# A fifth group of tiles in the first edges' matrix of a graph layer, and two buffers for its turned blocks

## The reference

```python
xn = _layernorm(x, axis=-1)
gathered = edge_vals[:, None] * x[cols]                              # x is xn, cols is dst
new_x = jax.ops.segment_sum(gathered, rows, num_segments=N_NODES)    # rows is src
out1 = new_x @ hamilton1        # batch norm, tanh, then @ hamilton2
```

## Time and profile before

| | us |
|---|---|
| runs, median of 3 | 2246.98 (2240.45 to 2256.11) |
| the profiled execution | 2244.61 |
| its span | 2243.2 |
| busy: PE, DVE, POOL, ACT | 1845.0, 1600.0, 1270.8, 1122.8 |
| scatters, all 566 | first issued at 95.7, last at 1265.1 |
| stage over the nodes, then experts | from 1269 to 1537, then to the end |

### The profile page before, as it was taken

The page is one execution under the profiler, slowest core; times in us unless marked ns, Lnnn a source line. Parts: engine busy times, 40 slices in busy tenths (PEclk is TensorE's granted clock), DMA queues, the critical chain, the costliest instruction groups (busy, mean ns, idle before and its releaser), DMA issues. The chain is left out here.

```text
span 2243.2 us, 36774 instructions
## 1 busy us (share of the span) xinstructions
PE 1845.0 (82%) x10829; PEld 1543.1 (69%) x10829; DVE 1600.0 (71%) x5189; ACT 1122.8 (50%) x2255; POOL 1270.8 (57%) x811
## 2 busy tenths in 40 slices
PE   3689996778788888878886287757999999999994
PEld 1366675566566666657775146635999999999994
DVE  4666667887877877853332196777888888888883
ACT  2544453222232333332222025348888988988983
POOL 1467787788877877877777400002544544554551
PEclk7599998888888989988998598857999999999997
DMA  9978877687788888889997771343888888888885
GB/s 316 353 132 170 157 118 125 111 127 127 125 166 148 143 175 147 154 171 189 178 181 120 144 252 60 122 142 85 240 228 240 227 231 241 226 233 236 232 234 159
DMA packets 326116, 401.84 MB, mean 179 GB/s; under 512 B 34999, under 2 KB 267468, under 8 KB 325778
## 3 DMA queue, kind: packets, MB, share of 16 engines
q1 hardware_dynamic: 194048, 257.05, 36.9%
q0 software_dynamic: 103008, 103.83, 34.6%
q10 hardware_dynamic: 28850, 38.50, 5.3%
HBM read 251.13 MB, written 154.55 MB: 181 GB/s over the span
## 5 line engine op out<-in xcount | busy, mean ns | idle before, releaser
L1143 POOL DMA_INDIRECT acc_dram<-third x566 | 905.3, 1599 | 275.3 <-issue 143.4
L2077 POOL DMA_INDIRECT sum_dram<-node,small x112 | 195.9, 1749 | 314.2 <-DVE node L2006 297.2
L563 PE MATMUL bank<-work,third 128*128 128x256 f32 x1132 | 308.3, 417 | 45.2 <-ACT third L1097 41.6
L1947 PE MATMUL bank<-down_parts 128*128 128x256 f32 x2688 | 335.4, 284 | 0.0
L1934 PE MATMUL bank<-up_parts 128*128 128x256 f32 x2688 | 333.1, 284 | 2.3 <-DVE up_parts L1964 2.3
L1934 PEld LDWEIGHTS bank<-up_parts 128*128 128x128 f32 x2688 | 327.9, 193 | 2.7 <-DVE up_parts L1964 2.7
L1947 PEld LDWEIGHTS bank<-down_parts 128*128 128x128 f32 x2688 | 325.3, 191 | 0.0
L1097 ACT ACTIVATE third<-bank 128x512 f32<-128x512 f32 x283 | 168.3, 597 | 287.0 <-DMA acc_dram<-third 219.9
L563 PEld LDWEIGHTS bank<-work,third 128*128 128x128 f32 x1132 | 228.2, 214 | 84.2 <-ACT third L1097 44.3
L2059 POOL DMA_INDIRECT node<-xh_dram,small x112 | 138.7, 1239 | 217.4 <-DVE small L1768 183.6
L1087 ACT ACTIVATE third<-bank 128x512 f32<-128x512 f32 (+1 forms) x142 | 84.7, 597 | 342.6 <-PE bank L552 337.6
(11 more groups left out here) (270 smaller groups left out, 2963.2 us busy)
## 6 DMA issues: line engine op xcount, KB each, us to landing
turned<-in_w_up SPq DMA_DIRECT2D x56, 1024.0 KB, 5.9
turned<-in_w_down SPq DMA_DIRECT2D x56, 1024.0 KB, 11.0
work<-src_dram SPq DMA_DIRECT2D x141, 256.0 KB, 4.2
acc_dram<-fixed SPq DMA_DIRECT2D x15, 1280.0 KB, 10.2
work<-xn_dram SPq DMA_DIRECT2D x146, 128.0 KB, 3.0
work<-acc_dram SPq DMA_DIRECT2D x72, 256.0 KB, 4.6
at_dram<-turned ACTq DMA_DIRECT2D x48, 256.0 KB, 4.2
work<-at_dram ACTq DMA_DIRECT2D x24, 512.0 KB, 4.5
```

The costliest lines, as they stand in the source:

```text
L563: k = e.matmul(bank[3 + h][:, (u - t) * D:(u - t + 1) * D], B[:, u % (2 * QUAD), :], win[:, q % 3, :], start=True, stop=True)
L1143: e.indirect_dma_start(acc_dram[i], bass.IndirectOffsetOnAxis(put_i[:, t:t + 1], 0), M[:, t % (ROW_QUADS * QUAD), :], None, compute_op=ALU ...
L1947: k = e.matmul(bank[5 + c][:, 0:D], hTs[:, hp, h, c * P:(c + 1) * P], W2s[:, 2 * b + wp, h, :], start=(h == 0 and hp == 0 and wp == 0), st ...
L2077: e.indirect_dma_start(sum_dram, bass.IndirectOffsetOnAxis(slot_i[:, n:n + 1], 0), yb[:, i % 2, c, :], None, compute_op=ALU.add).then_inc( ...
```

## The change

`DENSE` gets a fifth group, tiles 216 to 239 with `s` = 8. T0 becomes 240, so the scatter path has 542 tiles in place of 566 and 136 quads in place of 142. `NG` is 5, and by the line that was there already `AI` becomes 2. `HI * WIDEST` grows from 343 to 392 columns for the iota and the three buffers of `one_hi`. The room for it is found by making the row of zeros 320 floats long in place of 512 (each `fill` then writes 8 pieces of 1280 bytes per partition in place of 5 of 2048), while region `work` grows by 89 words, and the tables in it move. `group_i`, `offset_i` and `xn_group` grow with the group.

The plan is worked out anew from the same lines: the sum of costs is 608.0 over 136 quads. The keys lie beside the first 28 quads, the preparation ends at quad 32, the dense steps lie beside quads 31 to 107, the products beside quads 108 to 131, and nothing beside the last four. Before, a quad took 4.17 of cost; now it takes 4.61.

```diff
-DENSE = ((0, 108, 5), (108, 152, 6), (152, 188, 6), (188, 216, 7))
+DENSE = ((0, 108, 5), (108, 152, 6), (152, 188, 6), (188, 216, 7), (216, 240, 8))
@@
     AI = 3 if NG <= 4 else 2
-    assert ACC_ROWS * D // P // 512 % 5 == 0
+    ZW = 320
+    assert ACC_ROWS * D // P // ZW % 5 == 0 and ZW >= D + 4
@@
-        fixed = region("fixed", 4 * P + 512 + 8 * KC + 16 + 6 + P + HI * WIDEST)
+        fixed = region("fixed", 4 * P + ZW + 8 * KC + 16 + 6 + P + HI * WIDEST)
...
-        zeros = fixed(512)
+        zeros = fixed(ZW)
@@
-        work = region("work", 13064, late)
+        work = region("work", 13065 + 88, late)
@@
         early_end = 2 * CT * D + 2 * QUAD * P + 2 * P + 2 + 2 * P + EG * P + 2 * P + 2
+        work(88)
+        early_end += 88
@@
-            PIECE = ACC_ROWS * D // P // 512 // 5
+            PIECE = ACC_ROWS * D // P // ZW // 5
...
-                rows = acc_dram[i].rearrange("(p r) d -> p (r d)", p=P).rearrange("p (a b) -> p a b", b=512)
+                rows = acc_dram[i].rearrange("(p r) d -> p (r d)", p=P).rearrange("p (a b) -> p a b", b=ZW)
                 e.dma_start(rows[:, j * PIECE:(j + 1) * PIECE, :],
-                            zeros.unsqueeze(1).broadcast_to((P, PIECE, 512))).then_inc(s_acc0[i], 16)
+                            zeros.unsqueeze(1).broadcast_to((P, PIECE, ZW))).then_inc(s_acc0[i], 16)
```

## The result

| | before | after |
|---|---|---|
| runs, median | 2247.56 us (4 runs, 2240.45 to 2256.11) | 2290.48 us (4 runs, 2285.51 to 2296.86) |
| ratio, 95% interval | | 1.0181 (1.0149 to 1.0213) |
| first / last scatter | 95.7 / 1265.1 | 98.2 / 1298.3 |
| first dense tile | 409.3 | 401.4 |
| first product | 1012.3 | 1066.3 |

What follows compares the result with a forecast made beforehand. POOL was taken as the bound, with PE and DVE having 3% to give in the dense stage. +3 - 15 + 42 - 34 + 10 + 3 = +9 us gave 2256 us; range 2212 to 2284, the forecast's own 2234 to 2284.

Steps and rivals of the forecast that it cites:

- What bounds the kernel: Scatter loop: POOL is the bound; PE and DVE barely run ahead, with 3% to give in the dense stage.
- 18 of slack: Dense stage: PE and DVE gain 9 ready tiles on POOL in 605 us, 9 * 2.03 = 18 us.
- The start: Fills before the first scatter: smaller pieces of 1280 bytes cost +3 us, from nothing to +5.
- the +1 named beside it: Fills at the start: +1 us, estimated from the Trainium skill's fixed cost of some 3 cycles a packet.
- The keys' stage: Tiles of keys beside 28 quads in place of 31: -15 us, between -24 and -8.
- The dense stage: 24 tiles and 13 turning steps come in, DVE gets 39 us, PE 34: the stage grows by 42 us.
- they overlap perfectly: Dense stage: new DVE and PE work overlap with each other and nothing else, so it grows by 39 us.
- in the same waits as the old work: Dense stage: new work meets the same waits as the old, so it grows by 50 us.
- Products and tail: First product to last scatter: 17 fewer scatters -34 us, first chunk +10, loads +3.
- starved first chunk and the loads: Products' stage: POOL idles while PE waits for and multiplies the first chunk, +10 us; larger loads of `at_in`, +3.
- Rival 1: Dense stage: PE's clock rises, the chain absorbs the new work, POOL stays the bound; 2202 us, chance 0.2.
- Rival 2: Products' stage: two buffers for turned blocks make PE wait for loads, +27 us on the sum, 2283 us; chance 0.2.

Runs made afterwards that it cites:

- e_scatters_only: Kernel before with the last 24 tiles of edges left out of the scatters, no fifth group added: 2213.46 us, ratio 0.9849.
- The corners: Dense stage with 142 and 136 quads: 603.0 and 582.5 us without the fifth group, 675.5 and 664.9 us with it.
- e_phase_after: Kernel after the change, with DVE's own part of a quad moved between the two halves of its mixer steps: 2222.63 us, ratio 0.9842 to the kernel before.
- e_phase_before: Kernel before, with DVE's own part of a quad moved between the two halves of its mixer steps: 2240.89 us, ratio 0.9954.
- e_two_buffers: Kernel before with two buffers of turned blocks in place of three (`AI = 2`), nothing else: 2256.02 us, ratio 1.0015.
- e_g1_both: Kernel after, tiles 4 to 107 without one_lo blocks, one_hi blocks 4 and products 8 columns wide: 2273.73 us, ratio 1.0102 to the kernel before.
- e_zero_row: Kernel before with only the shorter row of zeros (320 floats) and 88 words more in the work region: 2253.19 us, ratio 1.0042.

## Why the prediction was wrong, point by point

- **What bounds the kernel: right, and it carried the case.** POOL paces and PE and DVE have little to give. With a third bank or the engines in step the stage of before stays at 603.2 and 602.1 us although the ring is full, so POOL sets it alone there; and with six quads fewer (e_scatters_only) it takes 582.5 us with 1 to 7 tiles ready, so the chain was close behind. Those 20.5 us are near the 18 of slack that I had read from the counts, but no measure of it: quads fewer also take their own work off the chain.
- **The start: right.** +2.0 and +2.5 us where +3 was taken; the +1 named beside it was too small. The rate at 50 to 60 us is 388 GB/s, between the 366 that I worked out and the 398 before.
- **The keys' stage: about right.** -10.4 for -15, inside its bounds.
- **The dense stage: the step that failed, +62 for +42.** Its amounts hold: DVE busy 499.4 for 461.9 us (+37.5, forecast 39), PE 519.2 for 489.9 (+29.3, forecast 34). PE's waits in the turning steps grew by 10.7 us (17.3 to 28.0) where 4 were in the sum. The price of the work, 39 to 50 us, was wrong, and I had marked it as the step I trusted least. I bounded it by "they overlap perfectly" (39) and "in the same waits as the old work" (50), both counted from DVE alone with PE beside it. The corners show 72 to 82 us for 37.5 + 29.3 us of work. A range up to the two engines' work added up, 39 + 34 = 73, would have held the 62, and the earlier trace rows gave reason for it: each engine waits 82 us for the other in 605, which two engines that overlap well don't do. But that sum is no law that the runs show: 82 is over it, and where 40 and 18 us of the two engines' work were cut, 6 came off. What they show in its place is that the price hung on the order of the work: the same group costs the dense stage 61.9 us as it stood, 22.4 with a third bank (603.2 to 625.6) and 12.4 with the engines in step.
- **Why the waits were there: not seen.** I took them for a property of the two banks. They came from the order: DVE's part of a quad and PE's stand two tiles apart, and each stops the other for up to 3.5 us. Both orders stood in the loops over `q`, and a timeline of the two engines side by side would have shown the 3 us stops. The move of one call shows it: it changes no work, buffer or bank, and takes 50.4 us off the stage, 20 us less of PE's busy time at the higher clock among its effects.
- **Products and tail: right in the sum.** 108 scatters in 232.0 us in place of 126 in 252.8; 18 fewer at 2.0 is -36 and the slower pace, 2.15 for 2.01 each, +15. Forecast were 17 fewer, -34, and +13 for the starved first chunk and the loads. PE did wait for that first chunk with few ready tiles to cover it (0 at 1040 us, 2 at 1080):

```profile
1066.26 6.93 PE L520 MATMUL bank<-work 128*128 128x256 f32 x20 [10.39 <-DMA work<-at_dram]
```

- **Rival 1 (the clock absorbs it)**: not in this kernel, 0.89 for 0.88. The clock has that gain to give, but the move brought it, and it was smaller than priced: 20 to 24 us of PE's busy time (e_phase_after, e_phase_before) where rival 1 had 37. **Rival 2**: out, by e_two_buffers and by the stage in which it had to show.
- **The rest of the 43 us.** The loop explains 33 in the profiles, which alone would have ended inside the range, at 2281. With +62 in place of +42, the sum would have been 2276. In the profiles the rest lies behind the loop, where other kernels vary by as much. But the stretch between `tanh` and the experts took over 184 us in 9 of the 12 kernels with the fifth group and in 2 of the 6 without it, so whether the 10 us that the medians show beyond the 33 are all chance wasn't settled.

What stays open: why cutting 40 us of DVE's busy time and 18 of PE's in the first group gave only 5.7 us, and what part of the 50 us is the clock's. That one engine's part stops the other is shown in the timelines and by the move; how a quad's 8.6 us split into the two parts and the steps from engine to engine for each tile was not measured apart.

## What to carry to other kernels

When two in-order engines share a small ring of buffers and each also has a lump of work of its own, find where the lumps stand in the common order: at different places, each lump can stop the other engine, and busy shares of 75 to 80% say nothing of room. Where the trace shows large mutual waits, let the range for new work on such a pair reach at least to the sum of both engines' work, and subtract only the slack that a count of ready items shows; here the same change lengthened the stage by 62 us in one order of the work and by 12 in another. Before buying more buffers, put the lumps at the same place.

## What the runs showed of the hardware

- The stretch from the start of the last `tanh` to the experts' first product has the same instructions in every kernel here and took from 170.0 us (e_g1_both; 170.1 in e_zero_row and e_phase_before) to 190.1 (e_two_buffers), 173.3 before and 186.0 after. Profiles of one part can so differ by 20 us, 0.9% of the kernel, without an edit that reaches it; a comparison of profiles should stop at the mark that the edit reaches.
- Less work went with a lower clock and hardly less time: in the first group PE's granted clock went from 0.87 to 0.83 when the products were cut to 8 columns, with 105 scatters in 230.1 and 224.4 us. And nearly the same busy share went with 0.89 in after (78% of 665 us) and with 0.95 in e_phase_after (81% of 614.5).
